# Two-layer graph network on one core: each gather of source rows waits for its own dense step of TensorE

## The reference, cut to what matters

```python
src = concat([s, d, loop]); dst = concat([d, s, loop])      # 212,500 edges over 12,500 nodes
o = argsort(dst, stable=True); src, dst = src[o], dst[o]    # sorted by destination
...
h = relu(layernorm(x))                                      # x: 12500 x 64
agg = segment_sum(h[src] + edge_attr, dst)                  # pass 0: messages with edge features
g = relu(agg @ W1 + b1) @ W2 + b2
x = x + batchnorm(g)
...
h = relu(layernorm(x))
h = relu(segment_sum((h @ V1)[src] * norm, dst) + c1)       # pass 1: GCN with self loops
h = relu(segment_sum((h @ V2)[src] * norm, dst) + c2)       # pass 2: the same with new weights
x = x + (h - mean(h)) / sqrt(var(h) + eps) * w + b
```

## Time and profile before

| | us |
|---|---|
| median of three timed runs | 2981.77 |
| lowest, highest | 2980.24, 2989.39 |
| span of the profiled execution | 4462.9 |
| TensorE busy in it | 3021.2 |
| VectorE busy in it | 1930.8 |
| GpSimd busy in it | 1887.0 |
| ScalarE busy in it | 795.8 |

### The profile page before, as it was taken

How to read it: one execution, slowest core, us unless ns; L and a number is a source line. 1 busy time by engine, 2 the same in 40 slices (tenths; PEclk the granted TensorE clock), 3 DMA queues, 4 the chain that set the end, 5 groups by cost and what they waited for, 6 DMA issues and landing times.

```text
span 4462.9 us, 66610 instructions
## 1 busy us (share of the span) xinstructions
PE 3021.2 (68%) x26545; PEld 2771.2 (62%) x26545; DVE 1930.8 (43%) x4856; ACT 795.8 (18%) x1708; POOL 1887.0 (42%) x1911
## 2 busy tenths in 40 slices
PE   1376666666766677737777777777857777777777
PEld 1265556666666566636667666666846766666667
DVE  9476667777777677742233332323301111111112
ACT  5122222222222223332111111111100000000000
POOL 6654444454454452033443344444144444444441
PEclk9987888888887788857787888887868878877788
DMA  4334333343434343343333333233453333333334
GB/s 118 84 101 110 98 100 112 97 116 101 115 100 114 96 116 104 111 125 120 113 100 113 113 112 130 88 129 115 149 127 127 112 122 118 113 124 113 112 128 124
DMA packets 341546, 504.30 MB, mean 113 GB/s; under 512 B 278786, under 2 KB 284344, under 8 KB 316401
## 3 DMA queue, kind: packets, MB, share of 16 engines
q1 hardware_dynamic: 280102, 402.60, 27.6%
q0 software_dynamic: 60512, 94.12, 9.8%
q10 hardware_dynamic: 616, 3.20, 0.3%
HBM read 362.65 MB, written 137.13 MB: 112 GB/s over the span
## 4 chain that ended last, share of the span: by engine, by line
PE 51%; another core or an unknown queue 16%; DVE 14%; issue 14%; ACT 2%; DVEq 1%; DMA 1%; SPq 0%; POOL 0%; ACTq 0%; POOLq 0%
PE psum L1105 34%; PE psum L1085 6%; DVE arena L958 4%; PE psum L1127 3%; PE psum L1120 3%; DVE arena L984 2%; DVE arena L955 2%; DVE arena L968 1%; PE psum L1068 1%; DVEq L1017 1%; ACT arena L1205 1%; PE psum L1140 1%; PE psum L1190 1%; PE psum L1186 1%
## 5 line engine op out<-in xcount | busy, mean ns | idle before, releaser
L1266 POOL DMA_INDIRECT arena<-table,srcT x1840 | 1799.8, 978 | 2248.8 <-PE psum L1127 1626.5
L1105 PE MATMUL psum<-arena 125*125 125x193 bf16 (+1 forms) x19200 | 2378.8, 274 | 385.6 <-issue 335.6
L1105 PEld LDWEIGHTS psum<-arena 125*125 125x125 fp8e4 x19200 | 2112.3, 157 | 491.6 <-issue 448.9
L1085 PE MATMUL psum<-arena 128*125 128x200 f16 x2272 | 609.4, 287 | 573.7 <-issue 290.0
L958 DVE TENSOR_SCALAR arena<-iota,keyT,oddT 128x200 f16<-128x200 f16 x2272 | 697.5, 335 | 601.3 <-remote 326.7
L1205 ACT CAST arena<-psum 125x400 uint16<-125x400 f32 x1136 | 548.8, 492 | 2131.8 <-PE psum L1085 1192.0
L1085 PEld LDWEIGHTS psum<-arena 128*125 128x125 f16 x2272 | 345.1, 157 | 660.5 <-issue 349.9
L955 DVE TENSOR_TENSOR arena<-modT,psum 128x500 f16<-128x500 f16 x568 | 376.3, 663 | 0.1
L1001 DVE TENSOR_REDUCE arena<-psum 125x64 f32<-125x192 f32 x192 | 67.2, 350 | 581.6 <-PE psum L1105 291.6
L968 DVE SCALAR_TENSOR_TENSOR arena<-relT,psum 128x960 bf16<-128x960 f16 x272 | 310.7, 1142 | 0.0
L984 DVE TENSOR_TENSOR arena<-arena 128x650 f32<-128x650 f32 (+1 forms) x334 | 274.4, 821 | 4.3 <-DMA arena<-in_edge_attr_dram 4.2
(11 more groups left out here) (217 smaller groups left out, 1037.0 us busy)
## 6 DMA issues: line engine op xcount, KB each, us to landing
arena<-counts SPq DMA_DIRECT2D x121, 1600.0 KB
counts<-arena SPq DMA_DIRECT2D x71, 1600.0 KB
arena<-in_edge_attr_dram SPq DMA_DIRECT2D x166, 320.0 KB
arena<-table,srcT POOLq DMA_INDIRECT x1840
table<-arena SPq DMA_DIRECT2D x8, 1050.0 KB
table<-arena SPq DMA_DIRECT2D x25, 168.0 KB
arena<-table SPq DMA_DIRECT2D x4, 1050.0 KB
arena<-in_x_dram ACTq DMA_DIRECT2D x4, 700.0 KB
```

Source lines behind the costliest of these rows:

```text
L1085: pe.matmul(to, ob(v // NB4 % NOB)[:, v % NB4, :], oh(v % NOH).rearrange("p (j m) -> p j m", m=2), start=True, stop=True).then_inc(p_bld, 1)
L1105: last = pe.matmul(ps_v[n % 2][0:PN, 0:xc], A(slot)[0:PN, j, 0:PN], Xs[0:PN, j, 0:xc], start=(j == 0), stop=(j == J - 1))
L1266: pool.indirect_dma_start(out=gbuf(slot)[0:parts, t, :], out_offset=None, in_=tables[k], in_offset=bass.IndirectOffsetOnAxis(ap=idx, axis= ...
```

## The change

`make_plan` now counts, for each gathered group and each of its ten gathers, how many app steps stand before a certain due time: GAT_LEAD = 2.2 intervals (of gathered groups) before the group for the first gather, and a tenth of an interval later for each next one. The last of the ten so has its place 1.3 intervals before the group. TensorE signals every app step but the last of a window on a new semaphore (24 of 25 steps, 4608 in all), and GpSimd waits before each gather until that many steps are signalled. Where the count is 0 there is no wait.

```diff
+GAT_LEAD = 2.2
...
+    steps = sorted(t for t, kind, v in pe if kind == "app" and v[1] < NAP - 1)
+    apart = (total - first - 3) / len(groups)
+    gat_every = apart * len(groups) / max(1, len([g for g in groups if g in with_gather]))
+    pace = {}
+    for t, kind, n in pe:
+        if kind == "grp" and groups[n] in with_gather:
+            pace[n] = [len([s for s in steps if s < t - GAT_LEAD * gat_every + i * gat_every / NT]) for i in range(NT)]
...
                     if i == NAP - 1:
                         last.then_inc(p_app, 1)
+                    else:
+                        last.then_inc(p_step, 1)
...
             for t in range(nt):
+                if pl["pace"][pl["gats"][i]][t]:
+                    pool.wait_ge(p_step, pl["d0"] * (NAP - 1) + pl["pace"][pl["gats"][i]][t])
                 idx = srcT[:, t, g - G0:g - G0 + 1] if g < G else src_l[0:R, t:t + 1]
```

## The result

The changed kernel takes 3003.24 us in the median of five runs (3000.09 to 3009.83), the kernel before beside it 2981.77 us (2980.19 to 2989.39, five runs): 1.0066 times as long, 95% interval 1.0047 to 1.0084. It is slower by 21.5 us; the forecast was 3001 us, 19 more than before.

The account below looks back on a forecast made before the run. In pass 2 GpSimd's gathers were taken as the bound, 12.49 us a group against TensorE's 11.6. A first gather 20.6 us later, other parts near nothing, taken as 19 us on 2981.8, gave 3001 us; range 2968 to 3035.

Parts of the forecast that it names:

- The bound of pass 2: Pass 2: GpSimd needs 12.49 us for a group of ten gathers, TensorE 11.6, so GpSimd sets the end.
- The term of the sum: Start of pass 2: the first gather waits for 21 steps and goes out 20.6 us later than before.
- go in whole: End of pass 2: GpSimd sets it before and after, so all 20.6 us of the late start are lost.
- The sum of 19 rather than 22 us: Whole kernel: 19 us added to the median, since the other end of the interval is +3.
- Waits and increments at nothing: Satisfied waits on GpSimd and 4608 increments on TensorE cost 0; waits for slot and step 2 us in pass 2.
- slower by more: Gathers of pass 2, perhaps pass 1: step waits lengthen the pitch by 0.05 to 0.1 us; 3028 to 3055 us, chance 0.10.
- the one on increments: Dense matmuls: increments cost TensorE time where it is the bound; 3103 us, chance 0.02.
- Passes 0 and 1 at nothing: Passes 0 and 1: pacing is worth 0, gathers already nearly even and later ones hidden behind the 4-slot buffer.
- The sign: Profile after, passes 0 and 1: gathers about 2 us apart instead of 1.25 in tens.
- The rebuilt sum: Timed kernel before, rebuilt from stretches with GpSimd idle: 2959 us, 23 below the median.
- the borders: Times before, between and after the passes, taken from the earlier profile: 310 us.
- The cause given for the holes: TensorE's pauses during gather bursts, 8.0 us each, 1481 us in all, belong to the slow profiled execution, not the timed runs.

Follow-up runs that it names:

- increments alone: The changed kernel with its step waits taken out and all 4608 increments kept; 2983.74 us, 0.9995 times the kernel before.
- free start: The changed kernel, but the first forty gathers of pass 2 wait for no step; 0.7794 times the kernel before, on another chip 1.0064.
- the longer first wait: The changed kernel with only one wait left, the first gather of pass 2, for 60 signalled steps instead of 21; 4484.83 us, 1.0059 times before.
- the last run: The changed kernel, in pass 2 first forty gathers without step waits, lead 3.6 intervals, groups 0.43 steps further apart; 2986.03 us, 1.0001 times before.

## Why the prediction was right, and where it wasn't

**The bound of pass 2: right.** TensorE's interval was taken as 11.6 us and is 11.62; GpSimd's as 12.49, and is 12.48 to 12.51. That the timed kernel before already waits at the end of pass 2 (14 us expected) holds: 11.0 us in five waits, the first at group 33, in the profile with increments alone.

**The term of the sum: right in mechanism and size.** The first gather goes out 19.95 us later counted from the table's store (20.6 predicted); the group at the end moved by 18.7 us; "go in whole" is so. The operand's pieces came 2.7 us sooner (2 predicted). One step was not seen: even without the first wait, the lead of the later waits takes the head start again. The sum of 19 rather than 22 us was a hedge and no reading; the medians gave 21.5. The chain of gathers moved by 18.5 us at its last gather in the first profile of the change, where its pitch is 1.248 us instead of 1.251, and by 20.0 us in the second, where both have 1.251.

**Waits and increments at nothing: right.** Gathers of pass 2 are (2954.23 - 2293.85) / 529 = 1.248 us apart with the waits and (2936.28 - 2274.45) / 529 = 1.251 without. The gathers that wait for a slot and a step stand 1.25 us behind their predecessors like the others; the 0.04 us that the prediction gave them came from no row, and the 2 us don't exist. So the rival "slower by more" falls by its own row, and the one on increments by its experiment.

**Passes 0 and 1 at nothing: right on chips of the first kind**, 0.9996. Pass 0's interval was sized too small (15.0 us; it is 15.9). The sign that the prediction gave for it, gathers "about 2 us apart", was wrong: in pass 1 most stand 1.25 us apart, 54 of 531 pitches are over 1.4 us and none is over 3, as its own 95% should have told it.

**The rebuilt sum: right in total only.** 310 us for the borders are 263, since the earlier trace rows has 47 us of starving in the first 190; pass 0's 1226 are 1286, pass 1's 752 are 742, pass 2's 671 are 697 of which 12 to 14 were counted apart. These errors partly cancel, to 2988 against 2959. The stretch without gathers didn't stand for pass 0: with increments alone a dense matmul comes every 0.239 us while gathers run there and every 0.221 us after them.

**The cause given for the holes: wrong.** The step that failed is "the profiled execution is slowed by 1481 us that the timed runs don't have": it took the profiler for the cause, "the bursts are the slow profile's". Timed runs on the chip of the second set take 4456 us, and the profiles there have the same holes. Profiles on the other chips show gathers 1.25 us apart through all of pass 2, with no pause between the tens, and no holes. So for pass 2 it was right that bursts with pauses between them belong to the slow profile, but they follow from the holes, which put TensorE's groups 21 us apart and let GpSimd wait for its buffers. What differs lies in the chip, or in what was going on in it. The conclusion drawn for the timed runs at hand, 2981.77 us and so free of holes, held all the same, because it rested on the rebuilt sum and the median and not on the cause. For a chip of the second kind a forecast of 19 us more would very likely have been wrong in sign: the nearest kernel that ran on one, the change with a free start, takes 0.7794 times the kernel before. No chance was kept for that.

**What stays open.** Why TensorE is starved there. Shown are: it happens from about 5 us into a burst of ten gathers to 3 us after the issue of the last one; the tenth gather of a burst costs 1.1 us; and it falls as the gathers are spread (342 us of "issue" to 84). That TensorE's instructions come late from memory, behind the gathers' small packets, would fit "issue" as the releaser, but the 16 KB packets of the queue of kind "instruction" take the same 1.05 to 1.1 us on both kinds of chip. There are some 330 packets of that kind in a whole execution, and with the longer first wait TensorE pauses 686 times for over 0.2 us with "issue" as the end, so not every pause can be one packet that comes late. No run here tested it. Whether it is the piece of silicon or its condition at the time can't be told from these chips. The kernel of the last run costs nothing on the first kind; what it or the unaltered change takes on the second wasn't measured.

## What to carry to other kernels

Before evening out a stream of transfers, compare its rate with its consumer's: where it is the slower one (12.5 against 11.6 us a group here), every microsecond of head start is worth about one at the end, until something else sets the end, and a late first wait and a short lead each take it. When a profile spans far more than the timed runs, find one that agrees with them before reading the change in it, and reckon with chips on which the long one is what the timed runs take too. What frees a late stage also moves its next transfer forward; look at what that meets.

## What the runs showed of the hardware

- One program, the kernel before: 2982 to 2986 us in the timed runs of the result and of three sets of experiments (each set on its own chip), 4456 us on the chip of the fourth set. TensorE gets through four matmuls every 2.13 us in a burst of indirect gathers on the latter, where it takes 0.086 us a matmul on the former (80 in 6.85 us). The profile before the change, a launch of its own, showed the same at 4462.9 us.
- Spreading the gathers is worth 22% on that chip (0.7794, with a free start of pass 2) and nothing on the others (0.9996 in the passes where they don't bound).
- The longer time there is not idle time alone: in 1200 us of pass 1 TensorE is idle for 330 us more and busy for 220 us more than in the 650 us that the same work takes elsewhere, at a mean granted clock of 0.79 instead of 1.00.
- A wait on GpSimd that is already satisfied leaves the pitch of gathers at 1.25 us, even two of them.
- A wait of 2 to 5 us on TensorE can be followed by a stretch at the 1.2 GHz level: 20 matmuls in 3.03 us instead of 1.84. In the changed kernel it cost nothing on top, since the next gather set the time: two profiles, with 20.5 and 10.2 us at that level, take 642.9 and 644.7 us from group 0 to 52.
- A gather issued 0.6 us after a 3.1 MB load is used 10.8 us after its issue, and TensorE waits for it; with the load 8.3 us behind the gather it is 4.5 us.
